# A third tile for the gated units' products, and new numbers for the table that sets the order of four interleaved streams

## The chip, the cores and the metric

The kernel runs on 1 core of a Trainium2 chip. The metric is the device time of one execution in microseconds. Its matrix engine is called PE here (PEld is its loading of weights), the vector engine DVE, the scalar engine ACT, GpSimd POOL, and the engine that only starts transfers SP.

## What is computed

Four layers, each an attention over a short context and a feed-forward part, with a gated residual around each. The input is 4 batches of 1,024 rows of 256 numbers, the context has 154 rows per batch, and there are 16 heads of 16 numbers.

```python
x = x + tanh(g_xattn[0]) * linear_attention_with_exp_features(layernorm(x), ctx)
x = x + tanh(g_ffn[0])   * butterfly_ffn(layernorm(x))            # 256 -> 1024 -> 256, gelu
x = x + tanh(g_xattn[1]) * softmax_attention(layernorm(x), ctx, mask)
x = x + tanh(g_ffn[1])   * (x W + two of eight low-rank experts)(layernorm(x))
x = x + tanh(g_xattn[2]) * softmax_attention(layernorm(x), ctx)
x = x + tanh(g_ffn[2])   * bitlinear(gelu(bitlinear(layernorm(x))))  # values rounded to 8 bits
x = x + tanh(g_xattn[3]) * softmax_attention(layernorm(x), ctx, mask)
x = x + tanh(g_ffn[3])   * gated_experts(layernorm(x))            # silu(h1) * h3, two of eight experts
```

The last part, the gated units, matters most here. With the two chosen experts of each row and their weights:

```python
h1 = t @ w1.T + SCALING * (t a1) b1        # for each chosen expert
h3 = t @ w3.T + SCALING * (t a3) b3
act = silu(h1) * h3
out = sum over the two experts of weight * (act @ w2.T + SCALING * (act a2) b2)
```

## The kernel before, in words

The rows are split over four streams, s0 to s3, of 256 rows each. A stream takes its 256 rows of one batch through all eight parts, and then loads its rows of the next batch, four times in all. `turns` (a generator) lists for each stream its stages with what they need. One round of all four streams through one batch is called an iteration below.

**The order.** No engine's order is written by hand. `orders` builds one list of stages for each of PE, ACT, DVE, POOL and SP. It keeps a time at which each engine is free, the costs of the stages in ns from `parts`, and counts of shared places: four PSUM banks together for scores (`quad`), one tile for exponentials (`ET`), single PSUM banks, and the shared tiles of the gated units. At each step it takes, of the stages that could be next, the one with the least start time plus a number from the table `BACK` (per engine and stage name). `late` and `early` add what a stage waits for outside its own chain. Each engine then runs its list strictly in order, and waits on semaphores inside each stage.

**Fillers.** Where `orders` finds PE free for over 900 ns before the stage that it has just chosen, and a PSUM bank is free, it puts a stage `fill` into PE's list: matmuls of the identity with itself, whose results nobody reads (L820). Their number is 0.6 times the gap in ns, divided by 215. They are there once the butterfly weights are folded, at the start.

**The gated unit of a stream (stages mw, exa, h1, h2, hw, back, e3, f3).** 1,024 hidden columns are taken in eight blocks j of 128. For block j, PE's `h1` makes h1 and h3 of the first expert in a PSUM bank (L1244, L1245), ACT takes the tanh (L1468), DVE makes the product of both (`half`, L1874 and L1881) into the left half of `PW[j % 2]`. PE's `h2` then adds the difference to the second expert in the same bank (L1253), and ACT and DVE make the product again, into the right half. POOL's `hw` multiplies both halves by the experts' weights (L785) and adds them into `G[:, j, :]` (L787), which `f3` multiplies with w2 at the end (L1277, L1278). PE's `back` multiplies `PW[j % 2]` with a2 (L1262). There are two tiles PW, one in `s.xn` and one in the shared tile `gu`. DVE's `h1` of block j may write the tile only when `back` and `hw` of block j - 2 are done. These are the waits in `half`:

```python
if c == 0 and j >= 2:
    e.wait_ge(s.p_a2, C.at(s.p_a2) + j - 1)
    e.wait_ge(s.g_p, C.at(s.g_p) + 2 * (j - 1))
```

`G` is eight blocks of 256 columns at the start of the stream's buffer `R`, so that blocks 6 and 7 are the columns 1536 to 2047.

The attention stages in the rows below are: `sc` (L957, scores, with masks L962 or L966), `mx` on DVE (L1661, the maxima), `mt` (L975), `sts` (L1013, L1015), `s2` (L1036, L1039, and L1045 with the mask), `ex` on ACT (L1417), `pv` (L1056, L1064), `out` (L1103). `turn` is L904, `qp` L926, `norm` L1639 on DVE, `gelu2` L1816 and what follows on DVE, `mw` L1223, `exa` L1232, `tl` L1149, `lin` L1160.

Of the kernel before, what the change touches and what calls it, by code (L numbers as in the profile page):

```python
# [29 lines left out]
def build(nc, d, out):  # L30
# [5 lines left out]
    with ctx:  # L36
# [133 lines left out]
        for i in range(NS):  # L170
            s = Stream()
# [55 lines left out]
            s.PW = [s.flat, gu[:, 2048:2560]]  # L227
            s.EX = [w.rearrange("p (k n) -> p k n", n=128) for w in s.PW]
# [90 lines left out]
        def late(name, of, engine):  # L319

            if engine == "DVE" and name == "h1" and of[2] > 1:
                return [("back", of[2] - 2)]
# [10 lines left out]
        def early(name, of, engine):  # L333

            if name == "back":
                return "back", of[1]
            if engine == "DVE" and name in ("h1", "h2"):
                return "half", half(name, of[2])
            return ("bias",) if name == "bias" else None

        def turns(s):
# [32 lines left out]
            for b in range(4):  # L374
# [111 lines left out]
        BACK = {"PE": {"down": -293, "down_there": 961, "exa": -486, "gate1": 1037, "h2": -790, "mw": -45, "near":  # L486
# [3 lines left out]
                600, "turn": 43, "up": 234, "val": 223, "wide": -1626},  # L490
                "DVE": {"down": 54, "e3": -216, "exa": -3100, "f3": -1123, "gate1": 432, "gate3": 79, "gelu2": 2064,
                "h1": -107, "lin": 550, "no": 301, "norm": -138, "out": 40, "tern": 601, "top1": 370, "top3": 1054,
                "upt": -1191, "val": -210, "w1": -44, "wide": 283},
                "POOL": {"bias": 499, "down_there": 442, "hw": 144, "no": -167, "norm": -313},
                "SP": {"kvw": -987, "late": -1105, "masks": -51, "store": 1715}}

        def orders():
# [67 lines left out]
            while True:  # L565
# [11 lines left out]
                i, p = min(can, key=lambda c: (start(c[1]) + BACK[c[1][2]].get(c[1][1], 0),  # L577
# [104 lines left out]
        def pool_program(e):  # L682
# [99 lines left out]
            def hw(s, j):  # L782
                pw = s.PW[j % 2]
                e.wait_ge(s.d_g, C.up(s.d_g))
                e.tensor_tensor(pw, pw, MW[:, 2:4, :].rearrange("p a b -> p (a b)"), ALU.mult).then_inc(s.g_p, 1)  # L785
                e.wait_ge(s.g_p, C.up(s.g_p))
                e.tensor_tensor(s.G[:, j, :], pw[:, 0:256], pw[:, 256:512], ALU.add).then_inc(s.g_p, 1)  # L787
# [1267 lines left out]
```

## Time and profile before

| | |
|---|---|
| median of three runs | 2890.6 us (2889.76 to 2895.37) |
| the profiled execution | 2893.2 us, of which 2891.2 us are the span in the trace |
| PE busy | 2621.1 us, 91% of the span, 21,811 instructions |
| DVE busy | 1724.6 us, 60% |
| ACT busy | 1142.6 us, 40% |
| POOL busy | 939.1 us, 32% |
| granted clock of PE over the span | 0.984 of full speed |

PE's busy time has the fillers in it: 543 matmuls, 137.9 us. What is neither work nor filler is idle time. The sum of both is what a better order could win, as long as PE's own work is the same.

### The profile page before, as it was taken

What the parts mean: (1) busy time and instruction counts of PE and PEld (TensorE: products, weight loads), DVE (VectorE), ACT (ScalarE), POOL (GpSimd) and SP (SyncE); (2) the same over time, 40 slices, a digit from 0 to 9 for tenths busy, and PEclk for the clock granted to TensorE, in tenths of its full rate; (3) what the DMA queues carried; (4) which work ended last, traced back from release to release, by engine and by line L of the source; (5) the groups of instructions that cost most, each with busy time, mean ns of one, the idle gap of its engine ahead of it and who ended that gap; (6) DMA issues with size and microseconds to landing.
All of it is one profiled execution on the core that took longest, in us unless ns stands there. A gap on an engine that the chain in (4) does not pass through costs nothing.

```text
span 2891.2 us, 55150 instructions
## 1 busy us (share of the span) xinstructions
PE 2621.1 (91%) x21811; PEld 1739.4 (60%) x21811; DVE 1724.6 (60%) x4702; ACT 1142.6 (40%) x1853; POOL 939.1 (32%) x2408
## 2 busy tenths in 40 slices
PE   4889988899999998899999998889999999889999
PEld 3447654576676654466667664447667665446666
DVE  6753588855534568866434457985543456886532
ACT  4644535522234444542233543542323453553211
POOL 1022232243334323233333333233333332323333
PEclk8999999999999999999999999999999999999999
DMA  4020000000000000000000000000000000000000
GB/s 168 1 87 11 11 2 13 1 1 8 8 12 15 11 1 1 13 1 8 8 8 14 5 11 1 11 1 1 9 8 18 9 11 1 1 1 1 5 4 8
DMA packets 18733, 37.00 MB, mean 13 GB/s; under 512 B 3600, under 2 KB 13872, under 8 KB 17456
## 3 DMA queue, kind: packets, MB, share of 16 engines
q1 hardware_dynamic: 18480, 33.48, 3.3%
q8 instruction: 176, 2.88, 0.4%
q14 instruction: 77, 0.63, 0.1%
HBM read 29.28 MB, written 4.19 MB: 12 GB/s over the span
## 4 chain that ended last, share of the span: by engine, by line
PE 65%; DVE 22%; issue 4%; ACT 4%; POOL 4%; SPq 1%; DMA 0%; DVEq 0%; POOLq 0%; ACTq 0%
PE P L1244 7%; PE P L1103 4%; PE P L1128 4%; PE P L1277 4%; PE P L1115 4%; PE P L1056 4%; PE P L1064 4%; DVE mx L1661 3%; PE P L1253 3%; PE P L1245 3%; PE P L1262 3%; PE P L1036 3%; PE P L957 3%; PE P L926 2%; PE P L833 2%
## 5 line engine op out<-in xcount | busy, mean ns | idle before, releaser
L1661 DVE TENSOR_REDUCE mx<-P 128x8 f32<-128x1232 f32 x256 | 367.9, 1437 | 239.6 <-PE P L962 83.9
L1244 PE MATMUL P<-xT,w 128*128 128x256 f32 x1024 | 269.8, 386 | 6.3 <-DVE xT L1703 5.1
L732 POOL TENSOR_TENSOR sm<-sm 128x2 f32<-128x2 f32 x384 | 77.0, 200 | 582.3 <-DVE sm L1657 561.9
L1712 DVE SCALAR_TENSOR_TENSOR x<-P,w_gates,x 128x512 f32<-128x512 f32 x112 | 83.9, 749 | 295.4 <-PE P L1278 123.5
L1417 ACT ACTIVATE ET<-P 128x2048 f32<-128x2048 f32 x96 | 180.1, 1876 | 193.6 <-PE P L1039 111.6
L1244 PEld LDWEIGHTS P<-xT,w 128*128 128x128 f32 x1024 | 192.9, 192 | 66.6 <-issue 19.0
L1370 ACT ACTIVATE xn<-x,sm 128x256 f32<-128x256 f32 x256 | 139.5, 592 | 207.7 <-POOL sm L740 207.2
L957 PE MATMUL P<-KB,R 32*128 32x308 f32 x1536 | 158.0, 469 | 49.2 <-ACT ET L1417 35.1
L1468 ACT ACTIVATE gu<-P 128x256 f32<-128x256 f32 x128 | 49.0, 383 | 372.6 <-PE P L1245 332.3
L1036 PE MATMUL P<-R,KB 32*128 32x256 f32 x2048 | 165.1, 409 | 9.3 <-DVE mx L1661 9.2
L785 POOL TENSOR_TENSOR xn<-xn,gu 128x512 f32<-128x512 f32 x64 | 81.1, 1268 | 256.4 <-DVE xn L1881 256.4
L1056 PE MATMUL P<-ET,VB 128*32 128x256 f32 x2048 | 138.1, 387 | 20.1 <-ACT ET L1417 12.4
L1245 PE MATMUL P<-gu,b 128*128 128x256 f32 x512 | 154.2, 383 | 0.0
L750 POOL TENSOR_TENSOR x<-x,w_bias 128x512 f32<-128x512 f32 x112 | 142.0, 1272 | 23.9 <-ACT xn L1370 23.5
L820 PE MATMUL P<-identb 128*128 128x512 bf16 x543 | 137.9, 382 | 0.0
L1253 PE MATMUL P<-gu,b 128*128 128x256 f32 x512 | 133.7, 384 | 4.4 <-DVE gu L1881 4.1
L957 PEld LDWEIGHTS P<-KB,R 32*128 32x128 f32 x1536 | 65.3, 183 | 111.3 <-issue 84.3
L1115 PE MATMUL P<-xT,wup 128*128 128x256 f32 x512 | 124.2, 386 | 2.2 <-issue 2.2
L1036 PEld LDWEIGHTS P<-R,KB 32*128 32x128 f32 x2048 | 82.5, 188 | 68.3 <-issue 35.1
L761 POOL TENSOR_TENSOR R<-R 128x256 f32<-128x256 f32 x48 | 35.3, 736 | 271.5 <-DVE R L1703 271.5
L1277 PE MATMUL P<-w_w,R 128*128 128x256 f32 x512 | 116.6, 381 | 2.0 <-DVE R L1897 1.3
L1874 DVE SCALAR_TENSOR_TENSOR gu<-gu,P 128x256 f32<-128x256 f32 x128 | 53.2, 416 | 109.3 <-ACT gu L1468 109.3
(302 smaller groups left out, 5797.8 us busy)
## 6 DMA issues: line engine op xcount, KB each, us to landing
kvw<-in_wkv SPq DMA_DIRECT2D x12, 672.0 KB, 4.0
x<-in_x SPq DMA_DIRECT2D x16, 256.0 KB, 2.8
out<-x SPq DMA_DIRECT2D x16, 256.0 KB, 2.1
w<-in_w SPq DMA_DIRECT2D x2, 1024.0 KB, 8.5
w<-in_wexp SPq DMA_DIRECT2D x1, 1028.0 KB, 7.3
w_w<-in_wcon SPq DMA_DIRECT2D x1, 1024.0 KB, 9.3
R<-in_m3t SPq DMA_DIRECT2D x1, 1024.0 KB, 10.9
R<-in_w1q SPq DMA_DIRECT2D x1, 1024.0 KB, 12.8
```

What stands on the lines that cost most here:

```text
L750: e.tensor_tensor(s.x[:], s.x[:], gb[:, k:k + 1, :].broadcast_to([128, 2, 256]), ALU.add).then_inc(s.g_x, 1)
L957: t = e.matmul(quad[:, g, 0:2 * NK], s.QT[G4[g], u, rows], K[G4[g], 2 * u:2 * u + 2, :], start=True, stop=l == 2)
L1036: e.matmul(quad[:, g, cols], K[G4[g], j, 0:128], s.QT[G4[g], j if l == 0 else u, :], start=a == 0, stop=False, skip_group_check=True)
L1056: t = e.matmul(bank[G4[q], 256 * z:256 * z + 256], main(z, q), ET[:, g, 256 * a:256 * a + 256], start=z == 0, stop=False, skip_group_check ...
L1115: t = e.matmul(o[:, 256 * (j % 2):256 * (j % 2) + 256], wup[:, c, 128 * j:128 * j + 128], s.xT[:, c, :], start=c == 0, stop=c == 1)
L1244: e.matmul(o, wm[:, c, js], s.xT[:, c, :], start=n == c == 0, stop=False, skip_group_check=True)
L1245: t = e.matmul(o, bm[:, js], U[:, 2 * n, :], start=False, stop=False, skip_group_check=True)
L1253: t = e.matmul(P[:, k, 256 * n:256 * n + 256], bm[:, js], U[:, 2 * n + 1, :], start=False, stop=n == 1, skip_group_check=True)
L1277: e.matmul(o, s.G[:, j, rows], w2[:, j, :], start=j == 0, stop=False)
L1370: t = e.activation(s.xn[:, i, :], s.x[:, i, :], ACT.Identity, bias=s.sm[:, 6, i:i + 1], scale=s.sm[:, 2, i:i + 1])
L1417: e.activation(ET[:].rearrange("p g c -> p (g c)"), quad.rearrange("p g c -> p (g c)"), ACT.Exp, bias=mb1[:, b:b + 1] if l == 1 else 0.0). ...
L1661: e.tensor_reduce(s.mx[:, i, :, 2 * u:2 * u + 2], quad[:, :, 0:2 * NK].rearrange("p g (a k) -> p g a k", a=2), AX.X, ALU.max).then_inc(q_d, 1)
```

## The change

1. `PW` gets a third tile, `R[1536:2048]` of the stream. This is where blocks 6 and 7 of `G` are written. DVE, POOL and PE use `PW[j % 3]`, and DVE's `h1` of block j waits for `back` and `hw` of block j - 3.
2. Since block 5 lies in the third tile (5 % 3 is 2), POOL's `hw` of block 6 waits for `back` of block 5 before its addition into `G[:, 6, :]`.
3. `late` and `early` tell `orders` these waits, and two that it had not been told: PE's `near` (the folding of the butterfly weights at the start) waits for DVE's `mat` of its number, and ACT's `mat` for the `near` four before.
4. All numbers in `BACK` are others, in larger sizes (up to 3,829 ns, where the largest was 3,100), and the choice adds 10 ns for each attention that the stream has behind it and 3 ns for the stream's number.

```diff
-            s.PW = [s.flat, gu[:, 2048:2560]]
-            s.EX = [w.rearrange("p (k n) -> p k n", n=128) for w in s.PW]
+            s.PW = [s.flat, gu[:, 2048:2560], part(1536, [512])]
+            s.EX = [w.rearrange("p (k n) -> p k n", n=128) for w in s.PW[:2]]
...
-            if engine == "DVE" and name == "h1" and of[2] > 1:
-                return [("back", of[2] - 2)]
+            if engine == "DVE" and name == "h1" and of[2] > 2:
+                return [("back", of[2] - 3)]
+            if name == "hw" and of[1] == 6:
+                return [("back", 5)]
+            if name == "near" and engine == "PE":
+                return [("mat", *of)]
+            if name == "mat" and engine == "ACT" and of[1] >= 4:
+                return [("near", of[0], of[1] - 4)]
...
+            if (name, engine) in (("mat", "DVE"), ("near", "PE")):
+                return name, *of
...
-        BACK = {"PE": {"down": -293, "down_there": 961, "exa": -486, "gate1": 1037, "h2": -790, "mw": -45, "near":
+        BACK = {"PE": {"exa": -581, "f3": 38, "gate1": -108, "gate3": -323, "h1": -1819, "h2": -3630, "key": -374,
...
-                i, p = min(can, key=lambda c: (start(c[1]) + BACK[c[1][2]].get(c[1][1], 0),
+                i, p = min(can, key=lambda c: (start(c[1]) + BACK[c[1][2]].get(c[1][1], 0) + 10.0 * count[c[0]] + 3.0 * c[0],
...
-                pw = s.PW[j % 2]
+                pw = s.PW[j % 3]
...
+                if j == 6:
+
+                    e.wait_ge(s.p_a2, C.up(s.p_a2, 8) - 2)
                 e.tensor_tensor(s.G[:, j, :], pw[:, 0:256], pw[:, 256:512], ALU.add).then_inc(s.g_p, 1)
...
-                e.matmul(o, a2[:, j, :], s.PW[j % 2], start=j == 0, stop=j == 7).then_inc(s.p_a2, 1)
+                e.matmul(o, a2[:, j, :], s.PW[j % 3], start=j == 0, stop=j == 7).then_inc(s.p_a2, 1)
...
-                if c == 0 and j >= 2:
+                if c == 0 and j >= 3:
 
-                    e.wait_ge(s.p_a2, C.at(s.p_a2) + j - 1)
-                    e.wait_ge(s.g_p, C.at(s.g_p) + 2 * (j - 1))
+                    e.wait_ge(s.p_a2, C.at(s.p_a2) + j - 2)
+                    e.wait_ge(s.g_p, C.at(s.g_p) + 2 * (j - 2))
```

Nothing of the work itself changes but two counts. PE's list has 357 filler matmuls in 78 places (543 in 118 before), and ACT's list has 65 loads of an activation table (107 before). Counted from the end of one round to the next, the fillers are 82, 79, 79 and 117 in the four iterations (131, 112, 112 and 188 before). In the last iteration, 38 of the 71 fewer lie in the last three gated units.

The new order at two places. The first is PE's list at the end of s1's last gated unit, where the last two `back` (L1262, after the change L1278), `h2` (L1253, then L1269) and the first matmuls of `f3` (L1277, then L1293) stand. L820 and L836 are the fillers. Before:

```order
3340 L1262 MATMUL P<-gu,w_a 128x512
3341 L820 MATMUL P<-identb 128x512 x4
3342 L1253 MATMUL P<-gu,b 128x256 x2
3343 L820 MATMUL P<-identb 128x512 x5
3344 L1262 MATMUL P<-xn,w_a 128x512
3345 L820 MATMUL P<-identb 128x512 x3
3346 L1262 MATMUL P<-gu,w_a 128x512
3347 L820 MATMUL P<-identb 128x512 x4
3348 L1277 MATMUL P<-w_w,R 128x256 x8
3349 L1278 MATMUL P<-w_b,R 128x256
3350 L1277 MATMUL P<-w_w,R 128x256 x8
3351 L1278 MATMUL P<-w_b,R 128x256
```

The same place after the change:

```order
3275 L1031 MATMUL P<-R,selt 64x256 x4
3276 L1029 MATMUL P<-R,KT 64x256 x4
3277 L1031 MATMUL P<-R,selt 64x256 x4
3278 L1037 MATMUL P<-mbT,identb 128x256 x4
3279 L1278 MATMUL P<-xn,w_a 128x512
3280 L1052 MATMUL P<-R,KB 128x256 x4
3281 L1055 MATMUL P<-R,sel 128x256 x4
3282 L1052 MATMUL P<-R,KB 128x256 x4
3283 L1055 MATMUL P<-R,sel 128x256 x4
3284 L1061 MATMUL P<-mbT,identb 128x256 x8
3285 L1278 MATMUL P<-gu,w_a 128x512
3286 L836 MATMUL P<-identb 128x512 x3
```

Matmuls of s3's last attention (L1029 to L1061) have taken the place of the fillers around the last two `back`. Its second half and `pv` follow, before s1's `f3`.

The second place is PE's list in the second iteration, behind an `out` of the second layer's attention (L1103, then L1119). Before:

```order
1215 L1103 MATMUL P<-w_wo,R 128x256 x4
1216 L820 MATMUL P<-identb 128x512 x3
1217 L957 MATMUL P<-KB,R 128x308 x4
1218 L962 MATMUL P<-onem,neg 128x308 x4
1219 L820 MATMUL P<-identb 128x512 x6
1220 L904 MATMUL P<-ident,xn 128x128 x4
```

After:

```order
1205 L1119 MATMUL P<-w_wo,R 128x256 x4
1206 L973 MATMUL P<-KB,R 128x308 x4
1207 L1029 MATMUL P<-R,KT 64x256 x4
1208 L1031 MATMUL P<-R,selt 64x256 x4
1209 L1029 MATMUL P<-R,KT 64x256 x4
1210 L1031 MATMUL P<-R,selt 64x256 x4
1211 L1165 MATMUL P<-ident,R 32x128 x2
```

The scores (L957) of the last stream stood alone behind `out`, with fillers on both sides. Now two streams further on stand close behind one another, and the fillers are gone.

## Rows read from the trace of the kernel before

**Rows 1.** The page's part 1: busy us, share of span, instructions.

```profile
PE 2621.1 (91%) x21811; PEld 1739.4 (60%) x21811; DVE 1724.6 (60%) x4702; ACT 1142.6 (40%) x1853; POOL 939.1 (32%) x2408
```

**Rows 2.** Issues of SP: stores of s0's rows, start, length, instruction.

```profile
1342.30 0.40 SPq L670 DMA_DIRECT2D out<-x  x1
...
2025.06 0.40 SPq L670 DMA_DIRECT2D out<-x  x1
```

**Rows 3.** Busy time by stretch: start and end, length, then each engine's busy us.

```profile
core 0: us, PE busy (x) PEld busy (x) DVE busy (x) ACT busy (x) POOL busy (x), PEclk, DMA share, GB/s
0.00:136.00 136.00, 93.39 (x722) 54.61 (x722) 93.92 (x243) 72.98 (x192) 16.49 (x49) 0.94 0.25 90
...
817.00:1498.00 681.00, 628.11 (x5368) 419.63 (x5367) 407.03 (x1110) 269.33 (x410) 232.98 (x598) 0.99 0.02 8
```

**Rows 4.** The same stretches, the fillers (L820) alone.

```profile
817.00:1498.00 681.00, 28.34 (x112) 10.10 (x112) 0.99 0.02 8
...
sum 2891.00, PE 137.85 PEld 49.88; mean PE 27.57 PEld 9.98
```

**Rows 5.** Busy time by stretch: the two halves of one iteration, columns as in Rows 3.

```profile
1012.00:1301.00 289.00, 250.99 (x2324) 153.60 (x2322) 218.40 (x609) 133.32 (x185) 88.64 (x277) 0.99 0.01 4
1301.00:1694.00 393.00, 378.24 (x3044) 266.75 (x3043) 187.87 (x501) 135.11 (x225) 143.79 (x321) 0.99 0.03 10
```

**Rows 6.** Timeline of PE, iteration 2 behind an `out`: start, length, idle before.

```profile
1053.52 0.81 PE L820 MATMUL P<-identb 128*128 128x512 bf16 x3
1055.04 0.80 PE L957 MATMUL P<-KB,R 32*128 32x308 f32 x8 [0.71 <-DVE mx L1661]
...
1055.90 1.47 PE L820 MATMUL P<-identb 128*128 128x512 bf16 x6
1058.49 0.66 PE L904 MATMUL P<-ident,xn 128*128 128x128 f32 x4 [1.12 <-ACT xn L1370]
```

**Rows 7.** Fillers by stretch at the end of s1's last gated unit.

```profile
2750.00:2800.00 50.00, 8.06 (x28) 2.96 (x28) 0.97 0.02 6
```

**Rows 8.** Timeline of PE at the same place: the steps with idle time before them.

```profile
2764.51 1.13 PE L1253 MATMUL P<-gu,b 128*128 128x256 f32 x4 [2.27 <-DVE gu L1881]
...
2772.09 3.72 PE L1277 MATMUL P<-w_w,R 128*128 128x256 f32 x16 [0.45 <-DVE R L1897]
...
2783.29 1.97 PE L1232 MATMUL P<-xT,w_a 128*128 128x256 f32 x8 [0.78 <-ACT gu L1463]
...
2786.64 1.13 PE L1244 MATMUL P<-xT,w 128*128 128x256 f32 x4 [0.30 <-DVE gu L1868]
```

**Rows 9.** Instructions of line 1881: who it waited for, who waited for it.

```profile
  PE P L1262: 71.5, 53
...
  PEld P L1253: 10.1, 15
  PE P L1253: 4.1, 6
```

**Rows 10.** Timeline of POOL at the very end: `hw` of block 6.

```profile
2873.98 1.27 POOL L785 TENSOR_TENSOR xn<-xn,gu 128x512 f32<-128x512 f32 x1 [2.25 <-DVE xn L1881]
2875.33 0.72 POOL L787 TENSOR_TENSOR R<-xn 128x256 f32<-128x256 f32 x1
```

**Rows 11.** Timeline of PE at the very end: `back` of block 5.

```profile
2871.63 1.02 PE L1262 MATMUL P<-gu,w_a 128*128 128x512 f32 x2
```

**Rows 12.** Groups by line: a load of an activation table on ACT.

```profile
L1430 ACT ACT_TABLE_LOAD x37 | 47.5, 1283 | 0.7
```

**Rows 13.** Timeline of PE around a fall of its clock in iteration 2.

```profile
1212.69 1.24 PE L1036 MATMUL P<-R,KB 32*128 32x256 f32 x8 [2.44 <-DVE mx L1661]
```

**Rows 14.** Busy time by stretch around it, and in iteration 1; columns as in Rows 3.

```profile
1208.00:1212.00 4.00, 2.24 (x32) 1.13 (x30) 3.44 (x18) 1.64 (x3) 0.00 (x0) 1.00 0.00 0
1212.00:1216.00 4.00, 3.31 (x29) 2.06 (x30) 3.83 (x11) 0.00 (x0) 0.00 (x0) 0.57 0.00 0
...
434.00:506.00 72.00, 59.49 (x594) 32.25 (x595) 61.26 (x162) 38.93 (x48) 21.40 (x60) 0.93 0.04 13
```

More of the change, by code:

```diff
@@ L483, in turns @@
                 yield "store", s, b
-        BACK = {"PE": {"down": -293, "down_there": 961, "exa": -486, "gate1": 1037, "h2": -790, "mw": -45, "near":
[3 rows of a table removed]
[L490 to L495, printed above, removed]
+        BACK = {"PE": {"exa": -581, "f3": 38, "gate1": -108, "gate3": -323, "h1": -1819, "h2": -3630, "key": -374,
+                "lin": 606, "mw": -577, "near": 1, "out": -115, "pv": 90, "q1": 505, "q2": -100, "qp": -77, "st":
+                242, "sts": 30, "tl": 194, "tsum": -3734, "turn": -210, "up": 275, "upt": 557, "val": -2153, "w1":
[4 rows of a table added]
+                "val": 749},
+                "DVE": {"down": 3829, "e3": -3675, "exa": 1495, "f3": 989, "gate1": -741, "gate3": 398, "gelu2":
+                3393, "h1": 563, "h2": 258, "lin": 1056, "masks": 613, "mat": 178, "mx": 216, "near": 209, "no":
+                662, "norm": -539, "out": 864, "q1": 72, "split": -1986, "tern": -2704, "top1": 1109, "top3": 2187,
+                "tsum": 937, "upt": 343, "val": -2069, "w1": 174, "w2": -12, "wide": 370},
+                "POOL": {"bias": 3168, "down_there": -27, "key": 2585, "mw": -2660, "no": -847, "norm": -1261},
+                "SP": {"kvw": -442, "late": 3187, "masks": -1025, "store": 2345}}
         def orders():
@@ L1871, in half @@
             def half(s, j, c, n, k):
-                pw, t = s.PW[j % 2][:, 256 * c:256 * c + 256], s.SL[n % 2]
+                pw, t = s.PW[j % 3][:, 256 * c:256 * c + 256], s.SL[n % 2]
                 e.wait_ge(s.a_d, C.up(s.a_d))
```

7 rows, old and new, of the table BACK are left out of this document.

## The prediction

> **What bounds the kernel now.** I read the page's busy line first. PE is busy for 2621.1 us of 2891.2, DVE for 1724.6 [rows 1]. PE is the engine that has no slack over the whole, but its busy time is not all work: the fillers take 137.9 us of it [rows 4]. So PE has 2621.1 - 137.9 = 2483 us of work, and 408 us of the span are idle or filler. The change leaves the work alone and can only touch these 408 us.
>
> The next view is the busy time by stretch. Two stores of s0's rows, one iteration apart, are 682.8 us apart [rows 2]. One such stretch of 681 us has 628.1 us busy [rows 3], of which 28.3 are 112 fillers [rows 4]: 52.9 us idle and 28.3 filler, 81.2 us to be had. The start (136 us, before any filler) has 42.6 us idle [rows 3] under transfers and the folding of the weights. From 136 us on, idle and filler together are 2755 - (2621.1 - 93.4) + 137.9 = 365 us.
>
> Inside one iteration there are two halves [rows 5]. In the 393 us with the gated units and the first layer, PE is busy for 378.2, or 96%: PE-bound, with 15 us to be had. In the 289 us with the middle layers PE is busy for 251.0 with DVE at 218.4: neither is full, and each waits for the other in turn. This half holds 38 us idle, and 109 of the 112 fillers by the same view. The order matters here. Single gaps show it: behind an `out`, PE runs three fillers, waits 0.71 us for DVE's maxima, runs six fillers and waits 1.12 us for ACT [rows 6].
>
> **The change part by part.**
>
> *The fillers as a measure of the order.* A filler stands where the order leaves PE free for more than 0.9 us, one per 0.36 us of the gap (0.215 / 0.6). That is arithmetic of the kernel's own code and no time of the chip, so I price it from rows. One filler keeps PE busy for 137.9 / 543 = 0.254 us [rows 4]. With the idle time beside it, the gaps of rows 6 come to (0.81 + 0.71 + 1.47 + 1.12) / 9 = 0.46 us per filler, and those at the end of s1's last gated unit to (8.06 + 2.27 + 0.45 + 0.78 + 0.30) / 28 = 0.42 us [rows 7, 8]. The list after has 186 fewer.
>
> *The end of the program.* 38 of the 186 lie in the last three gated units. Before, s1's unit runs out with nothing beside it: 28 fillers around its last `back`, `f3`, `mw` and `exa`, 11.9 us with the idle time beside them. Afterwards 3 of them are left, since s3's last attention stands there. That attention is work which PE did before s1's `f3` in any case, so what it covers is gained. At 0.42 us the 38 would be worth 16 us. The attention's own `pv` has to wait for ACT there, so I take three quarters: **12 us**.
>
> *The four iterations.* 148 fewer fillers: 49 in the first, 33 in each other. Bounds: nothing, if each gap that the lists close is opened again elsewhere, and 148 x 0.46 = 68 us, if each closes with all its idle time. I take the fillers' own time, 148 x 0.254 = **38 us**. My reason lies in the trace: 112 fillers stand for 112 x 0.36 = 40 us of gaps that the order knew of, while 81.2 us are there [rows 3, 4]. Half of the idle time comes from short waits that the order does not see, and a list chosen by that same order does nothing about them. So I count what PE provably spends in fillers, and leave the idle time beside them.
>
> *The third tile.* DVE waits 71.5 us, in 53 waits, for `back` before its product [rows 9]. That sounds large, but PE waits only 10.1 + 4.1 = 14.2 us for this product [rows 9], since its list has `h1` of the next block to do meanwhile. So the tile's ceiling is 14 us in all. Its visible part, the fillers ahead of `h2` (8 before, none after), is in the 186 already. I add nothing.
>
> *The new wait on POOL.* `hw` of block 6 waits for `back` of block 5 before its addition. Queued behind it on POOL are `hw` of block 7 and the `norm` and `bias` steps of other streams, and DVE's `e3` and PE's `f3` wait for those sums. At the very end `back` of block 5 starts at 2871.63 and takes 1.02 us; `hw` of block 6 starts at 2873.98, and its addition at 2875.33 [rows 10, 11]. The multiplication alone (1.27 us) covers the `back`, with 2.7 us to spare. Cost: nothing. If `back` of block 5 stood behind another stream's work, it would cost at most that stage, some 2 us in each of 16 units, on an engine that is busy 32% of the time.
>
> *Table loads.* 42 fewer at 1.283 us [rows 12] are 54 us of ACT time. ACT is busy 40% [rows 1]. Most of those removed belong to the gelu of the first layer, in the half in which PE is 96% busy. Between 0 and 54 us I take 0, since that half has no idle time on PE to give back.
>
> *The clock, a rule against this change.* Fewer fillers leave PE quieter where a gap stays. In rows 14 the granted clock is 1.00 up to 1212 us and 0.57 in the next 4 us, so mostly the lower level, 1.2 GHz of 2.4. PE had been busy for 2.24 us of the 4 before, and had waited 2.44 us for DVE's maxima [rows 13]. The Trainium skill (TensorE: Matmul & The Clock Gate, What's actually happening) says that the low clock is the default and that only activity of the array lifts it. By that rule alone, taking 186 matmuls out of idle places would cost clock; by the row, what matters is that the gap goes with them. The sum holds if the gap goes.
>
> *The start.* The corrected waits of `near` and `mat` concern the 42.6 us idle of the start [rows 3]. Both orders keep s0's and s1's attention beside the folding, and the two chains of 56 products alternate in both. Between 0 and some 20 us (half of that idle time), I take 0.
>
> *Sum.* 12 + 38 = 50 us off. The profiled execution would go from 2893.2 to 2843, with a span of about 2841. It lies 2.6 us over the median of the three runs, which would go from 2890.6 to **2840.6 us**.
>
> **The rivals.**
>
> *The gaps close whole.* If idle time goes down in proportion to fillers, 365 x 186 / 543 = 125 us go: 2766 us. For it: at both places of the order shown, real work stands where filler and wait stood. Against it: in the middle half DVE is at 76% [rows 5] with long steps in line, and the largest gap of that half, at s2's `pv` beside s0's `gelu2`, has 15 fillers in both lists. Anything beyond 80 us gained counts here.
>
> *A part only.* The end's 12 us and little else, since the iterations' order stands on costs that are off by tenths of a microsecond: 6 to 20 us off, about 2877 us.
>
> *The lists do not do on the chip what they do on paper.* The idle time that the order does not see (81.2 - 40 = 41 us in an iteration) grows by as much as the planned part shrinks, 12 us in each: 2890 us, no change. For it: the numbers of the table were chosen for that order's costs, with larger values than before, which is how a list comes to rest on small differences of cost. Against it: in rows 6 and 8 the gaps that the order had planned were there on the chip, so a gap that is gone from the list should mostly be gone there too.
>
> *Slower: the clock.* Place: the middle half, four times 289 us. Fillers are fewer (59 for 72 around the quantised layer), the long waits for DVE's maxima and roundings stay, and PE falls to its lower level more often. Iteration 1 shows the size: 0.93 over 72 us [rows 14], against 0.99 in the middle half of iteration 2 [rows 5]. All four halves at 0.93 cost 4 x 289 x 0.06 = 69 us, so 2890.6 - 50 + 69 = 2910 us. It decides from a loss of 50 / (4 x 289) = 0.043 of the clock on, so a granted clock below 0.95 there. This is what the rule of the clock page gives if gaps stay while their fillers go. Against it: 0.93 stands where fillers are densest, so they do not prevent it; what sets it is the long wait.
>
> **How the numbers follow.** A difference of over 0.2% (5.8 us) is what a measurement of this kernel can tell. Chances: the forecast (20 to 80 us off) 0.60, the gaps close whole 0.12, a part only 0.10, no change 0.08, slower 0.10. So faster is 0.82, same 0.08, slower 0.10. The range has to hold 8 in 10. Its low end, 2792, is 98 us off, more than the 68 + 16 = 84 us to which the bounds of the two terms add up, and some way into the first rival. Its high end, 2885, leaves out no change and slower.
>
> **What the profile after would show.** The fillers are 357 and take 357 x 0.254 = 91 us. PE's busy time falls by about 47 us to 2574, with its work within a few us of 2483. One iteration falls from 682.8 to about 674 us. Of the three gated units at the end, two instead of three run out with nothing beside them, and ACT has 54 us less to do. The DVE waits for `back` go from 71.5 us to below 20. If the clock's mean over the span is below 0.97, the slower rival is at work. If the iterations stay at 682 us and only the end is shorter, the price of 0.254 us per filler is wrong. If the span falls by over 80 us, the idle time beside fillers went with them.

## The result and the profile after

The kernel after takes 2750.2 us (median of four runs, 2748.2 to 2758.7), the kernel before 2892.5 us in the runs made beside it (2889.8 to 2895.4). The ratio is 0.9514, with a 95% interval of 0.9491 to 0.9536: 142 us less. The forecast was 2840.6 us and its range ended at 2792. The direction was right and the size was not: 50 us were forecast. Two executions among the runs below had a far lower granted clock, one of a_notie (3305.6 us, clock 0.749) and one of before (10446.2 us, 0.596); no time or ratio here uses them.

The profiled execution took 2750.75 us. Part 1 of its page answers to [rows 1]; behind it are its span and mean granted clock:

```profile
PE 2553.4 (93%) x21625; PEld 1716.8 (62%) x21625; DVE 1709.7 (62%) x4702; ACT 1085.9 (40%) x1811; POOL 935.2 (34%) x2408
```

```profile
core 0: 2749.0 us, clock 0.989
```

The busy time of PE by stretch: the start, then from store to store of s0's rows (the first iteration, three whole ones, the end), answering to [rows 3]. Behind it are the fillers (now L836) in the same stretches, answering to [rows 4]:

```profile
0.00:136.00 136.00, 98.97 (x759) 56.22 (x760) 96.77 (x247) 76.79 (x199) 15.60 (x50) 0.95 0.25 90
...
1270.00:1920.00 650.00, 613.97 (x5335) 416.67 (x5335) 403.25 (x1110) 252.48 (x399) 232.89 (x598) 0.99 0.03 8
...
2570.00:2749.00 179.00, 171.91 (x942) 127.46 (x940) 77.09 (x213) 33.15 (x70) 62.42 (x94) 1.00 0.02 7
```

```profile
136.00:620.00 484.00, 20.68 (x82) 7.47 (x82) 0.98 0.05 19
620.00:1270.00 650.00, 19.87 (x79) 7.26 (x79) 0.99 0.03 8
1270.00:1920.00 650.00, 19.86 (x79) 7.26 (x79) 0.99 0.03 8
1920.00:2570.00 650.00, 19.86 (x79) 7.27 (x79) 0.99 0.02 7
2570.00:2749.00 179.00, 9.67 (x38) 3.72 (x38) 1.00 0.02 7
sum 2749.00, PE 89.95 PEld 32.97; mean PE 14.99 PEld 5.50
```

An iteration takes 650 us where it took 683 [rows 2]. To see what went, I cut both spans at their own stores and split each stretch into idle time, fillers and work (busy time less fillers). The stretches of before come from the same view of that trace, cut at 136, 652, 1342, 2025 and 2707 us. (The cuts are at whole microseconds, so the stretches add up to the sums within 0.4 us; the sums are those of the whole span.)

| stretch | idle + fillers before | after | difference |
|---|---|---|---|
| start, 136 us | 42.6 | 37.0 | -5.6 |
| rest of iteration 1 | 57.1 + 31.6 | 46.5 + 20.7 | -21.6 |
| iteration 2 | 51.1 + 29.4 | 34.5 + 19.9 | -26.1 |
| iteration 3 | 52.8 + 28.3 | 36.0 + 19.9 | -25.3 |
| iteration 4 | 52.8 + 28.3 | 34.5 + 19.9 | -26.8 |
| behind s0's last store | 13.4 + 20.2 | 7.1 + 9.7 | -16.8 |
| sum | 408.0 | 285.6 | -122.4 |
| work, whole span | 2483.2 | 2463.4 | -19.8 |

The two sums give the 142.2 us by which the spans differ. Fillers are 47.9 us of it, which is what was priced. 74.5 us are idle time, of which the forecast counted only a small part, and 19.8 us are the same work in less time, which was expected to take as long as before.

**Where in an iteration.** The stores of the four streams show it. Issues of SP in one iteration, before and then after:

```profile
1426.54 0.38 SPq L670 DMA_DIRECT2D out<-x  x1
1503.23 0.38 SPq L670 DMA_DIRECT2D out<-x  x1
1587.10 0.38 SPq L670 DMA_DIRECT2D out<-x  x1
```

```profile
1269.77 0.40 SPq L683 DMA_DIRECT2D out<-x  x1
1339.68 0.38 SPq L683 DMA_DIRECT2D out<-x  x1
1409.79 0.38 SPq L683 DMA_DIRECT2D out<-x  x1
1478.70 0.38 SPq L683 DMA_DIRECT2D out<-x  x1
...
1920.13 0.40 SPq L683 DMA_DIRECT2D out<-x  x1
```

Before, s3's rows left 245 us behind s0's (1342.3 to 1587.1), now 209 us. The rest of the iteration is as long as ever, 438 and 441 us. Here are both parts in busy time, before and then after:

```profile
1342.00:1587.00 245.00, 235.12 (x1714) 171.09 (x1712) 107.47 (x284) 76.18 (x135) 92.25 (x178) 0.99 0.03 10
1587.00:2025.00 438.00, 395.07 (x3665) 250.02 (x3658) 299.85 (x828) 193.30 (x276) 141.01 (x422) 0.99 0.02 6
```

```profile
1270.00:1479.00 209.00, 208.62 (x1584) 153.11 (x1584) 108.24 (x284) 57.26 (x108) 84.62 (x158) 1.00 0.03 9
1479.00:1920.00 441.00, 405.35 (x3755) 263.56 (x3751) 295.01 (x826) 195.22 (x291) 148.27 (x440) 0.99 0.02 7
```

The stretch with the gated units had 9.9 us idle and has 0.4. It holds no filler in either kernel. It also has 26.5 us less of PE's busy time (235.1 to 208.6). The stretch in which PE waits for DVE took up 18.8 us of that: its work rose from 395.1 - 28.3 = 366.7 to 405.4 - 19.9 = 385.5 us while it became only 3 us longer. The other 7.7 us are work that took less time (601.8 us in the iteration before, 594.1 after). So most of the gain is work of PE that now lies inside the gaps of the other stretch, and idle time that is gone from the stretch with the gated units.

**Which gaps.** In the timeline of PE each step that waited carries its idle time. I added these up over one iteration (1342 to 2025 us before, 1270 to 1920 after), and set apart the waits that have a filler directly ahead of them or behind them. Those and the fillers themselves are taken as the gaps that the order marked:

| one iteration | before | after |
|---|---|---|
| fillers | 28.3 us, 112 | 19.9 us, 79 |
| idle beside a filler | 15.2 us in 18 | 11.3 us in 14 |
| idle with no filler beside it, up to 0.9 us | 17.5 us in 33 | 10.4 us in 22 |
| idle with no filler beside it, over 0.9 us | 19.2 us in 14 | 13.6 us in 10 |

(Waits below 0.15 us, 0.8 and 0.7 us in all, are left out.) Behind the first 136 us of the whole span, marked gaps fell from 137.9 + 74.8 = 212.7 to 90.0 + 47.8 = 137.8 us, and idle time with no filler beside it from 149.3 to 107.4 us. A marked gap is worth 0.39 us per filler in both kernels (212.7 / 543 and 137.8 / 357). Of the 41.9 us of unmarked idle time, 26 us come from the three stretches from s0's store to s3's (7.7, 9.9 and 9.9 us before, 0.4 us each after).

The longest wait before; then a short one and the longest after:

```profile
1864.38 0.90 PE L1194 MATMUL P<-identb,xn 128*128 128x128 bf16 x7 [2.93 <-DVE xn L1837]
```

```profile
1584.35 0.71 PE L1052 MATMUL P<-R,KB 32*128 32x256 f32 x8 [0.30 <-DVE mx L1677]
...
1744.92 1.07 PE L1072 MATMUL P<-ET,VB 128*32 128x256 f32 x16 [2.60 <-ACT ET L1433]
```

The 2.93 us have no filler beside them although they are over 0.9 us, and the 2.60 us have one directly ahead. So the length of a wait on the chip does not tell whether the order knew of it: a filler is put where the order's own reckoning leaves over 0.9 us, and part of a marked gap shows as a short wait behind its fillers, as in [rows 6].

**The two places of the order.** The end of s1's last gated unit, in the timeline of PE after, answers to [rows 7, 8]:

```profile
2623.31 1.02 PE L1278 MATMUL P<-gu,w_a 128*128 128x512 f32 x2
2624.17 0.81 PE L836 MATMUL P<-identb 128*128 128x512 bf16 x3
2625.44 1.07 PE L1072 MATMUL P<-ET,VB 128*32 128x256 f32 x16 [0.46 <-ACT ET L1433]
...
2630.73 3.62 PE L1293 MATMUL P<-w_w,R 128*128 128x256 f32 x16
```

Between `back` and `f3` stands s3's attention. From here up to the next `h1`, at 2642 us, PE has 3 fillers and 0.46 us idle, where 28 fillers and 3.8 us stood. Behind an `out` of iteration 2, answering to [rows 6], four stages follow with no gap at all:

```profile
1006.86 1.97 PE L1119 MATMUL P<-w_wo,R 128*128 128x256 f32 x8 [0.15 <-POOL R L774]
1008.75 0.80 PE L973 MATMUL P<-KB,R 32*128 32x308 f32 x8
1009.48 0.66 PE L1029 MATMUL P<-R,KT 32*64 32x256 f32 x8
...
1010.73 0.39 PE L1165 MATMUL P<-ident,R 128*32 128x128 f32 x2
1011.16 0.71 PE L1052 MATMUL P<-R,KB 32*128 32x256 f32 x8
```

### The profile page after: what moved, and what is told of

Same layout as the page of the kernel before. It is cut to its first block, busy times and chain, and to the rows that moved or that the text cites. A ratio compares the mean times of both kernels' runs of the same rounds, so it can differ in the third digit from the quotient of the medians.

```text
span 2749.0 us, 54741 instructions
## 1 busy us (share of the span) xinstructions
PE 2553.4 (93%) x21625; PEld 1716.8 (62%) x21625; DVE 1709.7 (62%) x4702; ACT 1085.9 (40%) x1811; POOL 935.2 (34%) x2408
## 4 chain that ended last, share of the span: by engine, by line
PE 69%; DVE 18%; ACT 5%; issue 4%; POOL 3%; SPq 1%; DMA 0%; DVEq 0%; ACTq 0%; POOLq 0%
PE P L1260 8%; PE P L1119 5%; PE P L1144 4%; PE P L1293 4%; PE P L1278 4%; PE P L1131 4%; PE P L1261 4%; PE P L973 4%; PE P L1072 4%; PE P L1080 4%; PE P L1269 4%; PE P L1052 4%; DVE mx L1677 3%; ACT ET L1433 3%; PE P L849 2%
## 5 line engine op out<-in xcount | busy, mean ns | idle before, releaser
L1260 PE MATMUL P<-xT,w 128*128 128x256 f32 x1024 | 264.0, 380 | 1.1 <-DVE R L1897 0.5
L973 PE MATMUL P<-KB,R 32*128 32x308 f32 x1536 | 163.6, 477 | 48.6 <-ACT ET L1433 27.3
L1072 PE MATMUL P<-ET,VB 128*32 128x256 f32 x2048 | 139.6, 391 | 20.2 <-ACT ET L1433 18.6
L1269 PE MATMUL P<-gu,b 128*128 128x256 f32 x512 | 132.1, 380 | 0.0
L774 POOL TENSOR_TENSOR R<-xT 128x256 f32<-128x256 f32 x48 | 34.8, 724 | 252.8 <-DVE xT L1719 252.8
L1052 PEld LDWEIGHTS P<-R,KB 32*128 32x128 f32 x2048 | 81.1, 185 | 59.1 <-issue 36.5
L1293 PE MATMUL P<-w_w,R 128*128 128x256 f32 x512 | 116.6, 381 | 0.9 <-DVE R L1913 0.9
L1144 PE MATMUL P<-wdn,R 128*128 128x256 f32 x512 | 113.8, 380 | 0.5
```

The costliest lines, as they stand in the source:

```text
L973: t = e.matmul(quad[:, g, 0:2 * NK], s.QT[G4[g], u, rows], K[G4[g], 2 * u:2 * u + 2, :], start=True, stop=l == 2)
L1052: e.matmul(quad[:, g, cols], K[G4[g], j, 0:128], s.QT[G4[g], j if l == 0 else u, :], start=a == 0, stop=False, skip_group_check=True)
L1072: t = e.matmul(bank[G4[q], 256 * z:256 * z + 256], main(z, q), ET[:, g, 256 * a:256 * a + 256], start=z == 0, stop=False, skip_group_check ...
L1144: t = e.matmul(o[:, 256 * i:256 * i + 256], s.hT[:, j, 128 * i:128 * i + 128], wdn[:, j, :], start=j == 0, stop=j == 7)
L1260: e.matmul(o, wm[:, c, js], s.xT[:, c, :], start=n == c == 0, stop=False, skip_group_check=True)
L1269: t = e.matmul(P[:, k, 256 * n:256 * n + 256], bm[:, js], U[:, 2 * n + 1, :], start=False, stop=n == 1, skip_group_check=True)
```

## The experiments

In all of them idle time, fillers and work are split as above, from part 1 of each page and the fillers' own sum. The table is in the order of time; the clock is the mean granted clock of the profiled execution. In the traces of seven kernels some records of the matmuls fed by `w1i` are missing, though their weight loads are there (26 in a_oldtable; 32 each in a_more, a_nonear, a_nohw6, a_two_re, b_newtable and a_zero). Put back, they would move an estimated 2 to 3 us from idle to work.

| kernel | us | fillers | their us | idle us | work us | clock |
|---|---|---|---|---|---|---|
| a_more | 2748.4 | 517 | 124.5 | 168.4 | 2457.2 | 0.993 |
| after | 2750.2 | 357 | 90.0 | 195.6 | 2463.4 | 0.989 |
| a_nonear | 2759.4 | 357 | 90.3 | 201.7 | 2465.6 | 0.986 |
| a_nofill | 2786.7 | 0 | 0 | 255.6 | 2529.4 | 0.963 |
| a_notie | 2792.4 | 436 | 110.3 | 208.2 | 2472.1 | 0.987 |
| a_nohw6 | 2852.5 | 558 | 140.9 | 231.3 | 2479.4 | 0.982 |
| b_three | 2888.6 | 543 | 136.8 | 264.5 | 2483.6 | 0.985 |
| before | 2892.5 | 543 | 137.9 | 270.1 | 2483.2 | 0.984 |
| a_two_re | 2916.2 | 597 | 151.5 | 261.6 | 2509.9 | 0.974 |
| a_oldtable | 2921.1 | 754 | 192.1 | 264.4 | 2466.5 | 0.987 |
| b_nofill | 2923.3 | 0 | 0 | 358.1 | 2560.6 | 0.957 |
| b_newtable | 2943.5 | 665 | 169.5 | 270.0 | 2518.0 | 0.971 |
| a_zero | 3033.5 | 971 | 242.1 | 309.2 | 2480.4 | 0.982 |

### b_three: the tile alone, on the lists of before

```diff
-            s.PW = [s.flat, gu[:, 2048:2560]]
-            s.EX = [w.rearrange("p (k n) -> p k n", n=128) for w in s.PW]
+            s.PW = [s.flat, gu[:, 2048:2560], part(1536, [512])]
+            s.EX = [w.rearrange("p (k n) -> p k n", n=128) for w in s.PW[:2]]
...
-                pw = s.PW[j % 2]
+                pw = s.PW[j % 3]
...
+                if j == 6:
+
+                    e.wait_ge(s.p_a2, C.up(s.p_a2, 8) - 2)
...
-                if c == 0 and j >= 2:
-
-                    e.wait_ge(s.p_a2, C.at(s.p_a2) + j - 1)
-                    e.wait_ge(s.g_p, C.at(s.g_p) + 2 * (j - 1))
+                if c == 0 and j >= 3:
+
+                    e.wait_ge(s.p_a2, C.at(s.p_a2) + j - 2)
+                    e.wait_ge(s.g_p, C.at(s.g_p) + 2 * (j - 2))
```

> The lists of the kernel before, word for word, with the third tile alone: DVE's h1 of block j waits for back and hw of block j - 3, and hw of block 6 waits for back of block 5. Theory 1 (the order made the gain, the tile only allows it): DVE's 71.5 us of waits for back shrink to under 20 us, but PE waited only 14.2 us for that product, so the time falls by 0 to 14 us against before (2890.6), ratio 0.995 to 1.0. Theory 2 (the tile itself carried a large part, since the half of an iteration with the gated units lost all its idle time, some 10 us in each): 25 us or more off, ratio 0.991 or lower.

Ratio 0.9985 (0.9971 to 0.9998): 4 us, as theory 1 had it. DVE's product (L1884 here) waits 0.5 us where it waited 71.5 [rows 9], and none of it for `back`. PE waits 3.0 us for the product, and its weight loads 8.2. An iteration still takes 682.6 us. The lines are "its engine sat idle before it", then "who waited for it", of that line:

```profile
its engine sat idle before it (us, times) until:
  DVE gu L1877: 0.5, 1
who waited for it (us, times):
...
  PEld P L1256: 8.2, 13
...
  PE P L1256: 3.0, 3
```

So 71.5 us of waits on DVE were worth 4 us, and the rest comes with the lists. That does not yet say what a third tile does for lists that are built for it: see a_two_re below.

### a_nofill and b_nofill: both kernels without fillers

```diff
-                if p[2] == "PE" and at - free["PE"] > 900.0 and done.get("folded") and let["bank"]:
+                if False and done.get("folded") and let["bank"]:
```

> The kernel after with its 357 filler matmuls left out of PE's list (their results are read by nobody), all else the same. Theory 1 (fillers are only markers of gaps; they neither cost nor buy time): within 6 us of after (2750). Theory 2 (they hold PE's clock up): 20 us or more slower than after, with a granted clock below 0.98 over the span. Theory 3 (some of them delay the next stage, being longer than the real gap): up to 10 us faster than after.

> The kernel before with its 543 filler matmuls left out. The same three theories: within 6 us of before (2890.6) if fillers only mark gaps; 30 us or more slower, with a granted clock well below 0.984, if they hold the clock up; up to 15 us faster if they delay what stands behind them. If removing 543 fillers changes nothing, then the 0.254 us that each keeps PE busy is no price of a gap at all.

The order of all stages is that of after and of before; only the fillers are left out. Spans and clocks, of a_nofill and then of b_nofill:

```profile
core 0: 2785.0 us, clock 0.963
```

```profile
core 0: 2918.7 us, clock 0.957
```

Without fillers, after is 36.5 us slower and before 30.8 us (32 and 30 us by the ratios to the runs of before made beside them). In a_nofill the work takes 66 us longer (2529.4 for 2463.4), while idle time is 30 us less than idle and fillers together were. So fillers are not lost time: the granted clock is higher with them, and they take about half of what they give (in b_nofill two thirds: the work is 77 us longer, for 50 us less of idle time and fillers). The granted clock has two levels, full speed and half of it, so a mean of 0.963 over 2785 us is 2 x 0.037 x 2785 = 206 us at the lower one, and in after 2 x 0.011 x 2749 = 60 us; the work takes 66 us longer for 146 us more at that level. The Trainium skill (TensorE: Matmul & The Clock Gate, What's actually happening) has the low clock as the default and activity as what lifts it; these two runs agree.

They also settle where the gain is. Without any filler the two spans still differ by 133.7 us, of which idle time is 358.1 - 255.6 = 102.5. The other 31.2 us are work, at clocks of 0.963 and 0.957. The fillers were a mark of the gaps, not the gain.

### a_more: more fillers in the same gaps

```diff
-                        lists["PE"].append(("fill", let["bank"][0][1], int(0.6 * (at - free["PE"]) / 215.0)))
+                        lists["PE"].append(("fill", let["bank"][0][1], int(0.85 * (at - free["PE"]) / 215.0)))
```

> The kernel after with 517 fillers instead of 357 in the same 78 places (0.85 of each gap instead of 0.6), nothing else changed. If the fillers hold the clock and there is more to be had (0.989 of full speed now), the clock goes to 0.993 or more and the time falls by some 10 us. If the gaps are full enough, the 160 more delay the work behind them: up to 160 x 0.254 = 41 us more, were none of them in idle time. If the gaps are long enough to take them in, the time stays within 5 us. I expect 0 to 15 us more.

2748.4 us against 2750.2, which no measurement here tells apart; 0 to 15 us more were expected, and this lies just under the lower end. The clock rose from 0.989 to 0.993 as the first of the three theories had it, but its 10 us did not come: work fell by 6.2 us, and idle and fillers together rose by 7.3 us (about 4 and 5 with the missing records put back). The 160 more fillers went into idle time, which the third theory had. So a count of fillers says nothing on the time by itself: it does so only at the same rule for setting them, as a measure of the gaps.

### a_notie, a_nohw6, a_oldtable, a_zero: other lists for the kernel after

a_notie leaves out the 10 and 3 ns, a_nohw6 the rule of `orders` that `hw` of block 6 waits for `back` of block 5 (the wait itself stays in the kernel), a_oldtable has the numbers of before in `BACK`, and a_zero none.

```diff
-                i, p = min(can, key=lambda c: (start(c[1]) + BACK[c[1][2]].get(c[1][1], 0) + 10.0 * count[c[0]] + 3.0 * c[0],
+                i, p = min(can, key=lambda c: (start(c[1]) + BACK[c[1][2]].get(c[1][1], 0),
```

> The kernel after without the two small terms in the choice (10 ns for each attention behind a stream, 3 ns for the stream's number). The lists come out differently, with 436 fillers in 95 places. Theory 1 (a filler less is worth its own 0.254 us, as predicted): 79 fillers more than after cost 20 us, 2770. Theory 2 (the filler count goes with the whole idle time, at the (2890.6 - 2750.2) / 186 = 0.75 us per filler of this case): 60 us, 2810.

```diff
-            if name == "hw" and of[1] == 6:
-                return [("back", 5)]
```

> The kernel after, whose orders is not told that hw of block 6 waits for back of block 5. The wait itself stays in the kernel, and the table is the same. PE's list then has 558 fillers in 120 places instead of 357 in 78. The theory that a filler stands for its whole gap: over the lists of the changed kernel with the same rules (357 fillers 2750, 436 fillers 2794, 754 fillers 2921, 971 fillers 3033 us) a filler is worth 0.43 to 0.56 us, so 558 give 2836 to 2862 us. The prediction's price (0.254 us, idle time beside the fillers left): 2750 + 201 x 0.254 = 2801 us. The theory that the lists matter little and this one wait alone matters (POOL waits now where it did not): 2750 to 2770 us, with a POOL wait for back at L803 of over 20 us.

```diff
-        BACK = {"PE": {"exa": -581, "f3": 38, "gate1": -108, "gate3": -323, "h1": -1819, "h2": -3630, "key": -374,
+        BACK = {"PE": {"down": -293, "down_there": 961, "exa": -486, "gate1": 1037, "h2": -790, "mw": -45, "near":
```

> The kernel after, three tiles and new rules, with the old table of numbers: 754 fillers. Theory 1: 397 more than after, 2851. Theory 2: 2968 to 3048. If the tile and the corrected rules were worth much by themselves, this would lie under 2890.

```diff
-        BACK = {"PE": {"exa": -581, "f3": 38, "gate1": -108, "gate3": -323, "h1": -1819, "h2": -3630, "key": -374,
+        BACK = {k: {} for k in ('PE','ACT','DVE','POOL','SP')}
```

> The kernel after with every number of the table at zero, so that the earliest possible stage is always next: 971 fillers. Theory 1: 614 more than after, 2906. Theory 2: 3088 to 3211. The difference to after is what the whole table is worth.

They took 2792.4 us (ratio to before 0.9649, 0.9631 to 0.9666), 2852.5 (0.9866, 0.9844 to 0.9888), 2921.1 (1.0109, 1.0081 to 1.0137) and 3033.5 (1.0492, 1.0463 to 1.0521). The table is worth 283 us against none at all, and leaving out the 10 and 3 ns alone costs 42 us. Three of the four lie between what their two theories gave (2770 and 2810, 2851 and 2968, 2906 and 3088 us), since the second theory had taken 0.55 to 0.75 us per filler.

These four give the price that the prediction had to choose. Idle time and fillers above the 285.6 us of after, by the fillers above its 357; then the marked gaps alone (fillers and the idle time beside them) above the 137.8 us of after:

| list | more idle + fillers | more fillers | us each | more in marked gaps | us each |
|---|---|---|---|---|---|
| a_notie | 32.9 | 79 | 0.42 | 27.6 | 0.35 |
| a_nohw6 | 86.6 | 201 | 0.43 | 74.3 | 0.37 |
| a_oldtable | 170.9 | 397 | 0.43 | 154.1 | 0.39 |
| a_zero | 265.7 | 614 | 0.43 | 245.7 | 0.40 |

Among lists made for three tiles, a filler stands for 0.43 us of all idle time and fillers, and for 0.35 to 0.40 us of its own marked gap. a_nohw6 was run to test it: 2836 to 2862 us were expected if a filler stands for its whole gap, 2801 by the prediction's price, and 2852.5 came. This is close to what the prediction read in [rows 6, 7, 8], 0.46 and 0.42, and not the 0.254 of the filler alone. From before to after it is (408.0 - 285.6) / 186 = 0.66 us, more than any of the four: those two differ in something that no filler marks. In a_nohw6 the theory that this one wait matters as such is out: POOL's addition waited for `back` once, 1.4 us. In the kernel after it did three times, 1.2 us in all; the view is that of the line of the addition:

```profile
its engine sat idle before it (us, times) until:
  PE P L1278: 1.2, 3
```

### a_two_re and b_newtable: the new numbers with two tiles

a_two_re is the kernel after with two tiles and the rules for two, its lists made anew. b_newtable is the kernel before with nothing changed but the numbers in `BACK`.

```diff
-            if engine == "DVE" and name == "h1" and of[2] > 2:
-                return [("back", of[2] - 3)]
-            if name == "hw" and of[1] == 6:
-                return [("back", 5)]
+            if engine == "DVE" and name == "h1" and of[2] > 1:
+                return [("back", of[2] - 2)]
...
-                pw = s.PW[j % 3]
+                pw = s.PW[j % 2]
```

> The kernel after with two tiles in place of three and the old rules for them in late (h1 of block j waits for back of block j - 2, hw of block 6 for nothing more), so that its lists are made anew with the new table: 597 fillers. Theory 1 (0.254 us per filler): 240 more than after, 2811. Theory 2 (0.55 to 0.75 us per filler, as the run without the small terms and the case itself gave): 2882 to 2930. Either way the question is whether the new table is worth anything with the rules of two tiles: under 2890 it is.

```diff
-        BACK = {"PE": {"down": -293, "down_there": 961, "exa": -486, "gate1": 1037, "h2": -790, "mw": -45, "near":
+        BACK = {"PE": {"exa": -581, "f3": 38, "gate1": -108, "gate3": -323, "h1": -1819, "h2": -3630, "key": -374,
```

> The kernel before, two tiles and old rules, with the new table: 665 fillers. Theory 1: 122 more than before, 2921. Theory 2: 2958 to 2982.

2916.2 us (1.0093, 1.0067 to 1.0119) and 2943.5 us (1.0197, 1.0144 to 1.025). Both are slower than before. The first is in its second theory's range and not under the 2890 that would have made the table worth something; the second lies between its two theories. DVE's product in a_two_re again waits for `back`:

```profile
its engine sat idle before it (us, times) until:
  PE P L1273: 66.6, 49
```

The two also show what the fillers left open. The idle time of PE with no filler beside it, in the three stretches from a round's first store to its fourth (these hold gated units), and behind the first 136 us in all:

| list | made by the rules for | unmarked idle in the three, us | marked gaps in the three, us | unmarked in all, us |
|---|---|---|---|---|
| before | two tiles | 7.7, 9.9, 9.9 | 1.4, 0, 0 | 149.3 |
| b_three | two tiles | 7.7, 9.8, 9.9 | 1.4, 0, 0 | 147.2 |
| b_newtable | two tiles | 9.0, 9.6, 9.1 | 1.0, 1.0, 1.0 | 151.7 |
| a_two_re | two tiles | 9.0, 9.7, 9.1 | 1.0, 1.0, 1.0 | 151.7 |
| after | three tiles | 0.4, 0.4, 0.4 | 0, 0, 0 | 107.4 |
| a_notie | three tiles | 2.9, 0.4, 0.4 | 4.3, 0, 0 | 113.1 |
| a_nonear | three tiles | 0.4, 0.4, 0.4 | 0, 0, 0 | 113.5 |
| a_oldtable | three tiles | 2.7, 2.3, 2.1 | 11.0, 10.0, 4.8 | 119.8 |
| a_nohw6 | three tiles | 1.3, 2.9, 2.2 | 6.0, 4.3, 6.0 | 120.3 |
| a_zero | three tiles | 1.7, 1.7, 1.8 | 3.0, 3.0, 3.0 | 126.9 |

The second of the three in a_two_re, which answers to the 209 us with 208.62 busy in after:

```profile
1329.00:1556.00 227.00, 216.95 (x1615) 154.82 (x1608) 105.70 (x291) 60.03 (x110) 89.68 (x173) 0.99 0.03 8
```

Whatever the numbers in `BACK`, lists made by the rules for two tiles leave 8 to 10 us of unmarked idle time there, and lists made by those for three leave 3 us or less. a_two_re differs from after in the tile and its rules alone. So this part of the gain comes with the third tile, but through the order: b_three has the tile with the old lists, and keeps the 9.9 us. The table has its share too. With the old one (a_oldtable) marked gaps of 5 to 11 us stand there instead, and in after none.

Set side by side: the tile without new lists gives 4 us, the new numbers without the tile cost 24 to 51 us, the tile and its rules with the old numbers cost 29 us, and all together give 142 us. Seen from after, the tile and its rules are worth 166 us with this table, and the table 171 us with this tile. The parts don't add up: the new table helps only the kernel that it came with, and even its small parts (a_notie, a_nohw6) cost 42 and 102 us when left out. How much of the 142 us another table for two tiles could have had stays open. The very lists of after with two tiles weren't tried: there the order of PE counts on the third tile being free, and engines could wait for each other in a circle.

### a_nonear: without the corrected waits of the start

```diff
-            if name == "near" and engine == "PE":
-                return [("mat", *of)]
-            if name == "mat" and engine == "ACT" and of[1] >= 4:
-                return [("near", of[0], of[1] - 4)]
...
-            if (name, engine) in (("mat", "DVE"), ("near", "PE")):
-                return name, *of
```

> The kernel after, whose orders is not told the two waits of near and mat at the start. Table, tiles and waits in the kernel are those of after, and the fillers are again 357. If the corrected waits at the start are worth something of the 42.6 us idle there, the first 136 us get longer and the time rises by up to 20 us. If they are worth nothing, as predicted, the time is 2750 us within 6 us, and the first 136 us have PE busy for 99 us within 2.

2759.4 us (2752.5 to 2759.5; ratio 0.9536, 0.9516 to 0.9556), 9 us over after, outside the 6 us expected, but the runs of both overlap. PE's list differs from that of after in a few rows at its very start only, and the other engines' lists are the same. The first 136 us hold 98.50 us of PE (98.97 in after), with a clock of 0.92 (0.95):

```profile
0.00:136.00 136.00, 98.50 (x752) 55.90 (x753) 95.65 (x245) 75.46 (x195) 15.50 (x49) 0.92 0.25 90
```

So these two rules are worth 0 to 9 us, and nothing tells which. Of the 5.6 us by which the idle time of the start fell they account for little: without them it is 37.5 us, for 37.0 in after and 42.6 in before. It goes with the table instead: b_newtable, which has no such rules, has 37.8 us there, and a_oldtable, which has them, 41.5.

## Why the prediction was wrong

**The step that failed** is the price of the four iterations: 148 x 0.254 = 38 us, with the words "leave the idle time beside them". They gave 21.6 + 26.1 + 25.3 + 26.8 = 99.8 us. That is two errors. The first: marked gaps go whole. The 148 fillers and the idle time beside them fell by 60.7 us, 0.41 us each. The prediction's own rows gave 0.46 and 0.42, and it used them for the end and not for the iterations. The second is the idle time with no filler beside it, of which it says that "a list chosen by that same order does nothing about them". That fell by the other 39 us. 26 of these lie in the stretches with gated units, and go with the third tile and its rules: the six lists made by the rules for three tiles have 3 us or less there in each, the four made by those for two 8 to 10. The remaining 13 us are unmarked waits of the other stretches, and no run shows what closed them.

**"In the half with the gated units there are 15 us to be had"** looked for the gain in the wrong way. Not only its own idle time counts: its work can be moved into the other half's gaps. Of the 26.5 us of busy time that left the stretch with the gated units, 18.8 us were moved, and that stretch is now without idle time.

**"Its work within a few us of 2483"** was 20 us off. The lists hold the same work, yet it took 2463.4 us. In the thirteen kernels the work goes with the granted clock, from 2457 us at 0.993 to 2561 at 0.957, some 29 us for each 0.01. That is 0.01 of the span. The time of repeats of one kernel goes the same way: b_newtable took 2959.6 us at 0.971 and 2938.9 at 0.980. Between before and after the clock rose by 0.005, which makes some 14 of the 20 us at that rate. The rest stays open.

**The end, 12 us**, holds. Behind s0's last store, idle and fillers are 16.8 us less. (The stretch is only 5 us shorter, since 11.8 us of work have moved into it.) 16 us, the sum before the discount of a quarter, would have been nearer.

**The third tile at nothing** was wrong, though its reading of the waits was right. With the old lists the tile gives 4 us, below the ceiling of 14 us. But that ceiling holds for the list of before, and not for one that is made for three tiles: there some 9 us of unmarked idle time go in each iteration.

**The wait on POOL at nothing** holds: 1.2 us in all. **The table loads at nothing**: ACT has 56.7 us less to do (1085.9 for 1142.6), about as said, but no run takes that apart from the rest. **The start at nothing**: 5.6 us less idle, which go with the table and not with the two rules.

**The rivals.** *The gaps close whole* was nearest: it forecast 125 us of idle time and fillers, and 122.4 came. In part that is luck. It let all idle time behind the first 136 us shrink by 186 / 543 = 34%, as the fillers do; marked gaps fell by 35%, but unmarked idle time fell by 28%, mostly for the reason above, which the rival did not name. Its time of 2766 was still 16 us too long, as it left out that the work would take less time. It had a chance of 0.12. What was held against it was DVE at 76% in the middle half; the stretch between s3's store and s0's took up 19 us more work all the same, with DVE busy for 295 us of its 441. *A part only* and *no change* are out: the planned gaps that were gone from the list were gone on the chip, and more. *Slower by the clock* is out: 0.989, above the 0.984 of before. It had the right mechanism for the wrong kernel, since a_nofill shows what leaving out the fillers costs where the gaps stay, 36.5 us. The gaps went with the fillers here.

Of the signs named, 357 fillers (90.0 us for 91), ACT, DVE's waits and the clock came as said. PE's busy time (2553 for 2574) and the iteration (650 us for 674) did not, and "if the span falls by over 80 us, the idle time beside fillers went with them" is what came.

## What to carry to other kernels

Price a marked gap by the whole gap in the trace, its padding and the idle time beside it. Then look at the idle time with no mark beside it by itself: a changed rule of the order (here a third buffer) can close it although no engine's wait for that buffer was worth much in the old order. Where two stretches have different bounds, count what can be moved from the full one into the gaps of the other, not only the idle time of each. Judge a table of priorities with all that came along with it: here each part alone gained 4 us or lost time.

## What was not expected of the hardware

Matmuls that nobody reads, set into gaps, are worth 30 to 36 us in a kernel of 2.8 ms, with a granted clock of 0.984 for 0.957 and of 0.989 for 0.963, though they take 90 to 138 us of PE. More of them raised the clock once more, to 0.993, and the time stayed. Across kernels, a mean clock lower by 0.01 went with some 29 us more of PE's work, and repeats of one program scatter by some 10 to 20 us, the longer ones at the lower clock (after: 2748.2 us at 0.988, 2758.7 at 0.986; b_newtable: 2938.9 at 0.980, 2959.6 at 0.971).
